# Expert results stored back per token inside the block loop, with the token and its weights carried in each row, and gate logits from raw transposed rows

## What is computed

```python
x = x + _L0_gnn_ref(_layernorm(x), adj, ...)         # exp(cosine) attention under adj, projection
x = x + _L0_ffn_ref(_layernorm(x)[None], ...)[0]     # mixture of 16 experts, two for each token
x = x + _L1_gnn_ref(_layernorm(x), adj, ...)         # two steps of top-p attention and of adj
x = x + _L1_ffn_ref(_layernorm(x)[None], ...)[0]     # dense experts
```

```python
logits = einsum('bsd,de->bse', x, gate_w) + gate_b
probs = softmax(logits)
top_probs, top_idx = top_k(probs, 2)
top_probs = top_probs / sum(top_probs)
dispatch = sum(one_hot(top_idx, n_experts) * top_probs[..., None], axis=-2)
hidden = silu(einsum('bsd,edh->bseh', x, w1)) * einsum('bsd,edh->bseh', x, w2)
expert_out = einsum('bseh,eho->bseo', hidden, w3)
return einsum('bseo,bse->bso', expert_out, dispatch)
```

## Time and profile before

| | |
|---|---|
| median of 3 runs | 983.84 us (983.31 to 983.94) |
| profiled execution | 986.32 us, of it the span 984.7 |
| TensorE busy | 712.4 us (72%), 4701 matmuls |
| VectorE busy | 676.1 us (69%), 2155 instructions |
| ScalarE busy | 456.1 us (46%), 626 |
| GpSimd busy | 204.3 us (21%), 474 |
| moved by DMA | 41.58 MB |
| first graph layer | 0 to 164 us |
| gate of the last chunk, scatter, tables | 164 to 207 us |
| 31 expert blocks | 207 to 298 us |
| gathers, weights, sums | 298 to 346 us |
| second program block | 349.5 to 984.7 us |

### The profile page before, as it was taken

The page is one execution under the profiler, slowest core; times in us unless marked ns, Lnnn a source line. Parts: engine busy times, 40 slices in busy tenths (PEclk is TensorE's granted clock), DMA queues, the critical chain, the costliest instruction groups (busy, mean ns, idle before and its releaser), DMA issues.

```text
span 984.7 us, 14242 instructions
## 1 busy us (share of the span) xinstructions
PE 712.4 (72%) x4701; PEld 526.3 (53%) x4701; DVE 676.1 (69%) x2155; ACT 456.1 (46%) x626; POOL 204.3 (21%) x474
## 2 busy tenths in 40 slices
PE   4999997789990056799999985175685685567274
PEld 2455554379990033578788753063563563567143
DVE  6766775513332367877675149999999999995868
ACT  4877773033330024443444356565865775711141
POOL 3402132321106650000000003203313413400000
PEclk9999997789995567899999997576987877898588
DMA  8743000267861100000000000000000001101001
GB/s 154 128 67 59 11 22 17 97 179 223 237 197 48 48 20 1 1 1 2 1 2 1 2 1 0 1 2 0 1 3 0 2 1 42 46 1 29 0 1 43
DMA packets 46735, 41.58 MB, mean 42 GB/s; under 512 B 7264, under 2 KB 44000, under 8 KB 46656
## 3 DMA queue, kind: packets, MB, share of 16 engines
q0 software_dynamic: 11984, 16.65, 8.6%
q1 hardware_dynamic: 33376, 22.93, 8.0%
q10 hardware_dynamic: 1296, 1.05, 0.3%
HBM read 39.57 MB, written 9.44 MB: 50 GB/s over the span
## 4 chain that ended last, share of the span: by engine, by line
DVE 33%; PE 24%; ACT 3%; issue 3%; DVEq 1%; SPq 0%; DMA 0%; ACTq 0%
PE bank L1808 6%; PE bank L1754 6%; PE bank L1767 5%; DVE big L1341 4%; DVE cand L1272 4%; DVE rm L1173 3%; PE bank L1791 3%; DVE hacc L1267 3%; DVE big L1332 2%; DVE big L1329 2%; DVE cand L1290 2%; DVE top L1285 2%; ACT big L1622 1%; ACT big L1595 1%; PE bank L1948 1%
## 5 line engine op out<-in xcount | busy, mean ns | idle before, releaser
L1622 ACT ACTIVATE big<-bank 128x512 f32<-128x512 f32 x128 | 70.4, 595 | 95.5 <-PE bank L1791 94.9
L1791 PE MATMUL bank<-ident,big 128*128 128x128 f32 x512 | 81.1, 307 | 35.1 <-DVEq L1364 28.2
L1754 PE MATMUL bank<-kk,qq 64*128 64x512 f32 x256 | 82.9, 777 | 32.6 <-ACT big L1595 32.6
L1791 PEld LDWEIGHTS bank<-ident,big 128*128 128x128 f32 x512 | 62.5, 155 | 61.7 <-DVEq L1364 28.9
L1595 ACT ACTIVATE big<-bank,negm 128x2048 f32<-128x2048 f32 x32 | 62.7, 1959 | 68.4 <-DVE fsc L1368 50.6
L1341 DVE SCALAR_TENSOR_TENSOR big<-big,st 128x2048 f32<-128x2048 f32 x32 | 73.9, 2349 | 14.0 <-PE bank L1791 14.0
L1071 POOL TENSOR_SCALAR bt<-bt 128x1 f32<-128x1 f32 x16 | 3.0, 190 | 364.7 <-ACT big L1612 224.4
L740 PE MATMUL bank<-big,xn 128*128 128x512 f32 x128 | 64.0, 623 | 2.7 <-DVE big L491 2.7
L579 DVE TENSOR_TENSOR big<-big,bank 128x512 f32<-128x512 f32 x31 | 21.3, 688 | 64.3 <-ACT big L687 64.3
L724 PE MATMUL bank<-xnT 128*128 128x512 f32 x128 | 62.3, 611 | 2.1 <-DVE xnT L480 2.1
L1754 PEld LDWEIGHTS bank<-kk,qq 64*128 64x128 f32 x256 | 27.5, 231 | 65.4 <-ACT big L1595 40.3
(11 more groups left out here) (336 smaller groups left out, 1579.2 us busy)
## 6 DMA issues: line engine op xcount, KB each, us to landing
big<-in_L_ffn_w_dram SPq DMA_DIRECT2D x93, 128.0 KB, 2.8
big<-in_adj_dram POOLq DMA_DIRECT2D x8, 512.0 KB, 7.6
big<-xs_scratch POOLq DMA_DIRECT2D x31, 128.0 KB, 3.3
ys_scratch<-big SPq DMA_DIRECT2D x31, 128.0 KB, 3.2
kk<-in_adj_dram POOLq DMA_DIRECT2D x4, 512.0 KB, 8.2
qq<-in_adj_dram POOLq DMA_DIRECT2D x4, 512.0 KB, 10.0
xs_scratch<-hacc SPq DMA_DIRECT2D x9, 128.0 KB
res<-in_x_dram SPq DMA_DIRECT2D x4, 256.0 KB, 7.2
```

The lines of the kernel that those rows point to most:

```text
L1622: nc.scalar.activation(MT[:, 4 * q:4 * q + 4, s * P:(s + 1) * P], bank[:, 5 + q % 2, :].rearrange("p (j i) -> p j i", j=4), ACT.Copy).then ...
L1754: nc.tensor.matmul(bank[:, c, :], qq[lo:lo + DA, (g * G + s) * P:(g * G + s + 1) * P], kk[lo:lo + DA, c * CH:(c + 1) * CH], start=True, st ...
L1791: mm = nc.tensor.transpose(bank[:, 5 + q % 2, j * P:(j + 1) * P], mk[:, s, jt * P:(jt + 1) * P], ident[:, :])
```

## The change

- **Rows.** A row of `xs_scratch` is W = 132 floats: the normalised token, its number, its first expert, the first weight, and the second weight less the first. `xg` becomes a ring of two chunks (its producers wait for the scatter of the chunk two before). The padding rows carry a first expert of -1, weights of zero and a number that leads to unused rows.
- **Weights during the gating.** VectorE's new `pay` writes the four extra floats; the exponential is computed per chunk on ScalarE (`exp_of`). The computation of `got_at` after the tables is gone.
- **Gate logits from raw rows.** TensorE transposes `res` and not `xg`; logits are rstd times the raw logits, plus nmr times the column sums of the gate's weights (`csum`), plus the bias. In the turns: `turn_x` 4 to 2, `gate_logits` 5 to 3, VectorE's `gate` 6 to 4, `pay` at 5, `place` 7 to 6, TensorE's `rank` 6 to 5, ScalarE's `take_xgT` 5 to 3, ahead of `xg_of` at 4.
- **Block loop.** ScalarE issues the xs loads (the first four ahead of the loop, then that of block m + 3 in turn m, between the copy and the silu). VectorE's new `target(m)` computes from the loaded rows, six small operations, where each row's result goes and by what weight it is scaled. `take_y` scales with that weight in two halves. GpSimd stores each half with an indirect DMA to row token + 2048 k of `ys_scratch`. SP no longer stores.
- **Return.** When all are stored, SP loads 8 pieces of 256 KB with plain DMAs; VectorE adds without multiplying.
- **SP's list.** The first block's weights are loaded after two of SP's zeroed tails.

The diff, cut:

```diff
@@ -191,8 +191,9 @@
...
+W = D + 4
@@ -231,23 +230,33 @@
...
-xg = xa2
+(TOK, E0, W0, DW) = range(D, W)
+xg = xa2[:, :, :].rearrange("p t d -> p (t d)")[:, 0:2 * TPC * W].rearrange("p (t d) -> p t d", t=2 * TPC)
...
+xs_dram = nc.dram_tensor("xs_scratch", (E * REG + SB, W), F32).ap()
+ys_dram = nc.dram_tensor("ys_scratch", (2 * N + MB * SB, D), F32).ap()
+tail = hacc[:, :, :].rearrange("p t d -> p (t d)")[:, 0:2 * W]
@@ -283,25 +292,23 @@
...
-        def store(m):
-            sp.wait_ge(y_out, m + 1)
-            sp.dma_start(ys_dram[m * SB:(m + 1) * SB, :].rearrange("(p a) d -> p a d", p=P), yb[:, m % NB, :, :]
-                         ).then_inc(b_st[m % NB], 16)
...
         sp.wait_ge(tail_ready, 1)
         for e in range(0, E, 2):
             zero_tail(sp, e)
-        sp.wait_ge(block_ready, 1)
-        for m in range(MB):
+            if e == 2:
+                sp.wait_ge(block_ready, 1)
+                load(0)
+        for m in range(1, MB):
             load(m)
-            if m >= NB:
-                store(m - NB)
-        for m in range(MB - NB, MB):
-            store(m)
+        for k in range(NB):
+            sp.wait_ge(b_st[k], 32 * ((MB - 1 - k) // NB + 1))
+        for c in range(NC):
+            for k in range(2):
+                rows = ys_dram[k * N + c * CH:k * N + (c + 1) * CH, :].rearrange("(t p) d -> p t d", p=P)
+                sp.dma_start(yg[:, k, c * TPC:(c + 1) * TPC, :], rows).then_inc(b_got[c], 16)
@@ -343,29 +352,18 @@
         for c in range(NC):
             pool.wait_ge(pos_ready, c + 1)
+            pool.wait_ge(payload, c + 1)
             pool.wait_ge(xg_ready, (c + 1) * TPC)
             for t in range(c * TPC, (c + 1) * TPC):
                 for k in range(2):
-                    pool.indirect_dma_start(xs_dram, bass.IndirectOffsetOnAxis(pos[:, k, t:t + 1], 0), xg[:, t, :],
-                                            None).then_inc(scattered, 16)
-        pool.wait_ge(at_ready, 1)
-        pool.wait_ge(scattered, 2 * NT * 16)
-        pool.wait_ge(zeroed, 16 * (E + 1))
+                    pool.indirect_dma_start(xs_dram, bass.IndirectOffsetOnAxis(pos[:, k, t:t + 1], 0),
+                                            xg[:, t % (2 * TPC), :], None).then_inc(scattered[c % 2], 16)
         for m in range(MB):
-            at_ = bass.ds(pool.value_load(block_at[0:1, m:m + 1], min_val=0, max_val=E * REG), SB)
-            if m >= NB:
-                pool.wait_ge(t_done, m - NB + 1)
-            pool.dma_start(xs[:, m % NB, :, :], xs_dram[at_, :].rearrange("(p a) d -> p a d", p=P)
-                           ).then_inc(b_xld[m % NB], 16)
-        for k in range(NB):
-            pool.wait_ge(b_st[k], 16 * ((MB - 1 - k) // NB + 1))
-        pool.wait_ge(got_ready, 1)
-        for c in range(NC):
-            for t in range(c * TPC, (c + 1) * TPC):
-                for k in range(2):
-                    pool.indirect_dma_start(yg[:, k, t, :], None, ys_dram,
-                                            bass.IndirectOffsetOnAxis(got_at[:, k, t:t + 1], 0)
-                                            ).then_inc(b_got[c], 16)
+            pool.wait_ge(y_out, 2 * m + 2)
+            pool.wait_ge(dest_ready, m + 1)
+            for a in range(2):
+                pool.indirect_dma_start(ys_dram, bass.IndirectOffsetOnAxis(dest[:, m, a:a + 1], 0),
+                                        yb[:, m % NB, a, :], None).then_inc(b_st[m % NB], 16)
     @block.vector
     def _(dve):
@@ -433,18 +431,27 @@
...
+            dve.wait_ge(ln_ready, c + 1)
+            for i in range(TPC):
+                ch.mark(nc.vector.scalar_tensor_tensor(out=glb[:, i, :], in0=csum, scalar=nmr[:, c * TPC + i:c * TPC + i + 1],
+                                                       in1=gateb, op0=ALU.mult, op1=ALU.add))
...
         def gate(c):
...
             dve.wait_ge(gl_done, c + 1)
-            ch.link(nc.vector.tensor_tensor(
-                gl[:, ts, :], bank[:, 7, E:E + TPC * E].rearrange("p (t e) -> p t e", t=TPC),
-                bcast(gateb.unsqueeze(1), [P, TPC, E]), ALU.add))
+            ch.sync()
+            for i in range(TPC):
+                t = c * TPC + i
+                ch.mark(nc.vector.scalar_tensor_tensor(
+                    out=gl[:, t, :], in0=bank[:, 7, (i + 1) * E:(i + 2) * E], scalar=rstd[:, t:t + 1],
+                    in1=glb[:, i, :], op0=ALU.mult, op1=ALU.add))
+            ch.sync()
...
             ch.sync()
+            nc.vector.tensor_tensor(gsm[:, 0, ts], m8[:, ts, 1], m8[:, ts, 0], ALU.subtract).then_inc(l21, 1)
@@ -459,6 +466,20 @@
...
+        def pay(c):
+            ts = slice(c * TPC, (c + 1) * TPC)
+            rows = xg[:, (c % 2) * TPC:(c % 2 + 1) * TPC, :]
+            if c >= 2:
+                dve.wait_ge(scattered[c % 2], 16 * 2 * TPC * (c // 2))
+            ch.mark(nc.vector.tensor_copy(rows[:, :, TOK], tokf[:, ts]))
+            ch.mark(nc.vector.tensor_copy(rows[:, :, E0], idx[:, 0, ts]))
+            dve.wait_ge(e21, c + 1)
+            ch.link(nc.vector.tensor_scalar(gsm[:, 2, ts], gsm[:, 1, ts], 1.0, None, ALU.add))
+            ch.link(nc.vector.reciprocal(rows[:, :, W0], gsm[:, 2, ts]))
+            nc.vector.scalar_tensor_tensor(out=rows[:, :, DW], in0=gsm[:, 1, ts], scalar=-1.0, in1=rows[:, :, W0],
+                                           op0=ALU.add, op1=ALU.mult).then_inc(payload, 1)
@@ -507,12 +537,11 @@
...
-            if c == 1 and p == 4:
-                dve.wait_ge(ld_g, 32)
-                dve.wait_ge(b_upper, 2)
+            if c and p == 4:
+                gate(c - 1)
+            if c and p == 5:
+                pay(c - 1)
             if c and p == 6:
-                gate(c - 1)
-            if c and p == 7:
                 place(c - 1)
@@ -547,31 +577,32 @@
...
-        ch.link(nc.vector.tensor_reduce(shift, oh_all, AX_X, ALU.add))
-        ch.link(nc.vector.tensor_tensor(shift, shift, posf, ALU.add))
-        nc.vector.tensor_copy(got_at, shift).then_inc(got_ready, 1)
...
+        def target(m):
+            k, v = m % NB, xs[:, m % NB, :, :]
+            dve.wait_ge(b_xld[k], 16 * (m // NB + 1))
+            ch.mark(nc.vector.tensor_scalar(k1[:, m % 2, :], v[:, :, E0], rows_m[:, BE_, m:m + 1], None,
+                                            ALU.not_equal))
+            ch.link(nc.vector.tensor_scalar(t1[:, m % 2, :], v[:, :, E0], 0.0, float(SB * m), ALU.is_lt, ALU.mult))
+            ch.mark(nc.vector.scalar_tensor_tensor(out=dest0[:, m % 2, :], in0=k1[:, m % 2, :], scalar=float(N),
+                                                   in1=v[:, :, TOK], op0=ALU.mult, op1=ALU.add))
+            ch.link(nc.vector.tensor_tensor(wy[:, k, :], k1[:, m % 2, :], v[:, :, DW], ALU.mult))
+            nc.vector.tensor_tensor(dest[:, m, :], dest0[:, m % 2, :], t1[:, m % 2, :], ALU.add
+                                    ).then_inc(dest_ready, 1)
+            nc.vector.tensor_tensor(wy[:, k, :], wy[:, k, :], v[:, :, W0], ALU.add).then_inc(w_ready, 1)
         def take_y(m):
             dve.wait_ge(d_done, m + 1)
+            dve.wait_ge(w_ready, m + 1)
             if m >= NB:
-                dve.wait_ge(b_st[m % NB], 16 * (m // NB))
-            nc.vector.tensor_copy(yb[:, m % NB, :, :], bank[:, 6 + m % 2, 0:SB].rearrange("p (a d) -> p a d", a=2)
-                                  ).then_inc(y_out, 1)
+                dve.wait_ge(b_st[m % NB], 32 * (m // NB))
+            for a in range(2):
+                nc.vector.tensor_scalar(yb[:, m % NB, a, :], bank[:, 6 + m % 2, a * P:(a + 1) * P],
+                                        wy[:, m % NB, a:a + 1], None, ALU.mult).then_inc(y_out, 1)
+        target(0)
         for m in range(MB):
             dve.wait_ge(sil_done, m + 1)
@@ -581,15 +612,13 @@
...
+            if m + 1 < MB:
+                target(m + 1)
         take_y(MB - 1)
         for c in range(NC):
...
-                ch.mark(nc.vector.tensor_tensor(yg[:, k, ts, :], yg[:, k, ts, :],
-                                                bcast(gsm[:, 2 + k, ts].unsqueeze(2), [P, TPC, D]), ALU.mult))
-            ch.sync()
             ch.link(nc.vector.tensor_tensor(yg[:, 0, ts, :], yg[:, 0, ts, :], yg[:, 1, ts, :], ALU.add))
             nc.vector.tensor_tensor(res[:, ts, :], res[:, ts, :], yg[:, 0, ts, :], ALU.add).then_inc(b_x, 1)
@@ -616,8 +645,16 @@
...
-                nc.scalar.activation(xg[:, t, :], res[:, t, :], ACT.Identity, bias=nmr[:, t:t + 1],
+                if c >= 2:
+                    act.wait_ge(scattered[c % 2], 16 * 2 * TPC * (c // 2))
+                nc.scalar.activation(xg[:, t % (2 * TPC), 0:D], res[:, t, :], ACT.Identity, bias=nmr[:, t:t + 1],
                                      scale=rstd[:, t:t + 1]).then_inc(xg_ready, 1)
+        def exp_of(c):
+            ts = slice(c * TPC, (c + 1) * TPC)
+            act.wait_ge(l21, c + 1)
+            nc.scalar.activation(gsm[:, 1, ts], gsm[:, 0, ts], ACT.Exp).then_inc(e21, 1)
@@ -651,14 +688,17 @@
...
+            if c and p == 3:
```

(40 more changed lines are left out.)

63 lines of the change are left out of this document (33 added, 30 removed).

## The result

The changed kernel takes 953.28 us (median of 4, 951.56 to 955.32), the kernel before beside it 983.58: ratio 0.969 [0.967, 0.971], that is -30.3. The forecast was 953.8. The profiled execution took 951.56 us, the quickest of the four.

What follows compares the result with a forecast made beforehand. TensorE was taken to bound the first graph layer and expert blocks, GpSimd's 32 exposed gathers the return. Return -27.9, gate -1.5, first layer -0.6 and loop 0 gave -30.0: 953.8 us from the median 983.84, range 949.5 to 962.5.

Steps and rivals of the forecast that it cites:

- The return: After the last block: gathers replaced by indirect stores in the loop and plain loads, -27.9 us, limits -28.5 and -24.5.
- The block loop: The 31 expert blocks: added work on ScalarE, VectorE and GpSimd stays covered, 0 us, limits 0 and +3.
- rival (c): Block loop: xs loads from ScalarE's queue land late, +0.2 to +0.45 us a block, 960 to 968; chance 0.12.
- (a): Block loop: a store held by VectorE's product makes GpSimd the pace half way, +8 us, 962; chance 0.12.
- (b): Block loop: every store costs 2.01 + 0.30 beside VectorE's work, +55 us, about 1009, slower; chance 0.04.
- The gate: Last chunk's gating to block start: scatter 4.0 us earlier, of which 1.5 arrive at the first up projection, limits 0 and -4.
- The tails are not the limit: Block start: SP's zeroed tails, done at about 198.1, don't hold the first xs load, expected behind ScalarE's row sums at 199.3.
- The first layer: First graph layer: shorter one-hot wait -1.4, waits of 0.4 in two chunks +0.8; -0.6 us, limits -2 and +3.
- Rival (d): Around 160 us: fewer waits hold the upper clock longer, up to 3 us shorter, 951; chance 0.12.
- The sum: Whole kernel: -27.9 - 1.5 - 0.6 + 0 = -30.0 us, so 956.3 for the profiled run and 953.8 for the median.

Runs made afterwards that it cites:

- lock_sbuf: The changed kernel plus, ahead of each block's product on VectorE, a dummy product of two SBUF tiles; 967.30 us, one execution.
- after_again: The changed kernel measured again without edit, on the chip of the second measurement of the kernel before; 951.24 us beside 983.07 of before.
- before_again: The kernel before measured again without edit; 982.83 us beside 983.07 of before.
- gate_only: The kernel before plus only the gating part: raw rows transposed, logits put right on VectorE, new turns; 977.89 us, ratio 0.994.
- stores_only: The changed kernel without its gating part: logits from normalised rows in the old turns; 956.82 us, ratio 0.974.
- pool_first4: The changed kernel with the first four xs loads issued by GpSimd instead of ScalarE; 970.13 us beside 986.77 of before, ratio 0.984.
- pool_load: The changed kernel plus two 128x256 memsets on GpSimd behind each block's pair of indirect stores; 969.62 us, one execution.
- sp_loads: The changed kernel with SP's tails ahead of the weights, first four xs loads on GpSimd, the 27 others on SP; 971.86 us, ratio 0.985.
- both: The changed kernel with GpSimd issuing the first four xs loads and ScalarE loading block m + 4 behind block m's silu; 970.71 us, ratio 0.983.
- after_beside: The changed kernel repeated without edit on a third chip; 972.17 us beside 986.08 of before, ratio 0.984.

## Why the prediction was right, and where not

**The return: right, 1.7 too dear.** Forecast 20.2 from the last copy to the sums' end, measured 18.6. Landing and SP's start were 1.43 for 1.55. The mis-sized term is the transfer: 12.3 for the last of 2 MB and 2.35 behind it are 14.7, measured are 13.3. The first load landed 3.9 behind its issue, not 4.8, and but for 0.31 before the second chunk the others kept ahead of VectorE, which then needs 9.4 for four chunks, as the working had. So the bound was VectorE's, not the transfer's.

**The boundary: not in the sum.** -2.7. The prediction left this term out. I had subtracted 40.7 us of gathers from GpSimd's list and not asked what its last one still holds: the end of the program block, 8.49 behind it, 3.2 behind VectorE. Rows 2 end before this; the row of the next block's first instruction would have shown it.

**The block loop: right only where before takes 983.** 90.8 to 90.9 from up to out became 91.4 and 91.5, within 0 to +3; one late xs load is 0.43 of it, so rival (c) is true once in 31 blocks. On three other chips the stretch from up to the last store is 16 to 22 longer, outside every limit I gave for the loop. None of my rivals had it: it is not GpSimd's pace (a) nor the xs loads' reach (c) by the runs above.

**Rivals (a) and (b).** The 62 stores had a mean of 0.97, and 29 of them waited for VectorE. The mechanism of (b) exists, as lock_sbuf shows; it has no place here because the product and the scalings read PSUM. 27 stores of four profiles began inside the product of 0.69 and took 0.96 to 0.98. The trace agrees with what the Trainium skill, SBUF — State Buffer, "Who interferes with whom", ties the lock to, two SBUF inputs, and not with its inference that a product of tensors spares descriptor making.

**The gate: the path right, the start it was measured from wrong.** Forecast 4.0 gained by the scatter, of which 1.5 arrive. From the last gather of the layer to the last chunk's first scatter it is 18.4 (changed) and 18.0 (after_again) for 23.15 in before_again: 4.8 to 5.1 gained. Nothing arrives: up is 1.4 to 2.6 later. Four marks say why:

| run | SP's last tail out | first xs load | last row sum copied | up |
|---|---|---|---|---|
| before | 198.77 | 201.76 | 203.28 | 207.15 |
| before_again | 193.22 | 197.48 | 201.91 | 203.06 |
| gate_only | 189.11 | 193.37 | 197.91 | 199.06 |
| stores_only | 198.68 | 204.17 | 203.35 | 209.06 |
| changed | 192.75 | 200.42 | 199.61 | 204.43 |
| after_again | 193.88 | 201.65 | 200.84 | 205.67 |

The prediction's path is there: ScalarE's loads start 0.62 to 0.64 behind the end of its last row-sum copy in all seven profiles that have them on ScalarE, and its figure for up, 205.6, lies 0.1 from one profile and 1.2 from the other. The step that failed is the subtraction from 207.15. In that one profile the tails held the first load, and up stood 3.9 behind the row sums; in before_again and gate_only it is 1.15 behind them. So the usual kernel before loses nothing to its xs loads, and the changed one, with 4.8, loses 3.7 by putting them behind the row sums. The change of place is a loss, not a part of the gain. "The tails are not the limit" holds for the changed kernel; it fails for before's first profile and where GpSimd issues the first loads. The row sums themselves came 1.75 later behind the scatter than in before_again; in pool_first4, with the same list of TensorE, they did not (18.1), so that is a matter of the execution. My comparison with the first profile of before gave -2.7 and looked like a hit: that was luck.

**The first layer: the sign was wrong.** Forecast -0.6. From VectorE's first product with the adjacency to TensorE's last gather it is 136.9 in before, before_again and gate_only, and 137.8 in the changed kernel's two profiles: +0.9. (The start of the last gather alone says +0.5 to +2.3, but the first product stands anywhere from 23.5 to 25.1, without pattern.) The two sizes behind the forecast were both off. In gate_only, VectorE's gating in its new turns costs 0.8 in each of the second and third chunks, for 0.4, and the last chunk gives back 1.8, for 1.4. In the changed kernel they cost 0.9 each, and the last chunk gives back 1.0. What it has beyond gate_only is `pay`, `exp_of` and the ring of rows, to which the forecast gave no price in this layer; stores_only, with them and without the new turns, has 138.0. Which of the three it is was not tried. TensorE waits for VectorE's product at each chunk's end, here ahead of the last:

```profile
158.03 1.98 PE L794 MATMUL bank<-big,xn 128*128 128x512 f32 x4 [0.64 <-DVE big L512]
...
161.38 1.99 PE L794 MATMUL bank<-big,xn 128*128 128x512 f32 x4 [1.37 <-DVE big L512]
```

The wait of 2.07 for the one-hots did go; a step later VectorE is what is late.

**Rival (d).** In the first pair of profiles the clock in 160 to 164 us was 0.50 before and 1.00 after, and the stretch from the last gather to the layer norm's factors 2.9 shorter (11.2 for 14.1). before_again has 1.00 and 12.4 there, without the change: 1.7 of the 2.9 is a matter of the execution, not of the change.

**The sum.** Against before_again and after_again: up to out +0.8, return -29.7, boundary -2.7, start +2.6, the second block 635.3 in both; -29.0 for this pair of profiles, and -31.8 by the medians. Of the +2.6 at the start, 1.3 is the later first product of after_again (25.11 for 23.78). That 953.8 was met within 0.5 is partly luck. Boundary and return gave 4.4 more than forecast. The first layer and the block start, forecast at -2.1, cost 1.4 to 2.6 instead. In the first pair this second miss is hidden, because before's profile had its late block start, and 956.3 was forecast for a profile of 951.56.

## What stays open

Why the block loop stalls on some chips when the results go back by indirect stores. Shown: it is not GpSimd's work (pool_load); ScalarE's DMAs are not needed for it (sp_loads, in which late xs loads explain a part); one block more of reach doesn't help (both). Both kernels move about as much in the loop where before takes 983 (218 and 222 GB/s in 209 to 290 us), and on the other chips before loses 3 to 4 us where the change loses 20. In one stall that was read closely, the news of TensorE's work came 2.4 us late. Only argued: that the indirect stores themselves, or the number of semaphore updates that DMAs send in a block, meet something in those chips. before has no profile from such a chip, and stores two to a block without indices weren't tried.

No version was faster than the changed kernel by more than the spread. Tails ahead of the weights and the first loads on GpSimd put the block start 2.8 to 4.0 us earlier than in after_beside, but of this only 2.4 us was seen in time, inside the spread; that it is worth keeping is likely and not shown. Where before takes 983 neither was tried.

## What to carry to other kernels

Ask of work taken off an engine what its last instruction still holds: here the end of the program block was worth 2.7 us more. Take a second profile of the kernel before, ahead of reading differences of 2 us in one place: two of the same kernel lay 4.1 apart at the block start, and a forecast that was subtracted from the odd one looked right. Moving a load to another engine puts it behind all that stands in that engine's list: here 3.7 us. And a gain measured on one chip can be half on the next, so a change of what a loop stores and how wants a second chip.

## What the hardware showed unexpectedly

- An indirect DMA of 0.97 us that begins inside a VectorE product of two SBUF tiles ends 0.84 us behind that product, if its own 0.97 doesn't reach further, with a product of 1.23 us (before) as with one of 0.69 (lock_sbuf); beside a product with an input from PSUM it isn't touched (27 stores).
- GpSimd's side of a program block closes 8.49 us after its last indirect gather (three profiles), 10.2 with a wait for the landing (one).
- The same kernel took 951 us on one chip and 972 on another, and the kernel before 983 and 986.
- Eight tails of one kernel's list took SP 11.7 us to give out in one execution and 8.1 in another.
